# Factorization-machine kernel: squares and their weighing one quad later, and a ring of 6 quads instead of 8

## The reference

```python
gathered = jax.vmap(lambda table, idx: table[idx], in_axes=(0, 1), out_axes=1)(emb, xi)
e = gathered * xv[:, :, None]
s = jnp.sum(e, axis=1)
qi = 0.5 * (s * s - jnp.sum(e * e, axis=1))
h = jax.nn.relu(xv @ W1 + b1)
x = jnp.concatenate([qi, h], axis=1)
return x @ W2 + b2
```

## Time and profile before

| | |
|---|---|
| median of 3 runs | 752.67 us (750.71 to 755.29) |
| the profiled execution, its own time | 753.14 us |
| its span, first to last instruction | 751.3 us |
| gathers on GpSimd | 512, 508.3 us busy |
| scales on ScalarE | 512, 323.1 us busy |
| squares on ScalarE (L194) | 66, 224.7 us busy |
| weighings on VectorE (L327) | 128, 276.8 us busy |
| HBM read | 131.72 MB, 175 GB/s over the span |

### The profile page before, as it was taken

How to read it: one execution, slowest core, us unless ns; L and a number is a source line. 1 busy time by engine, 2 the same in 40 slices (tenths; PEclk the granted TensorE clock), 3 DMA queues, 4 the chain that set the end, 5 groups by cost and what they waited for, 6 DMA issues and landing times.

```text
span 751.3 us, 2355 instructions
## 1 busy us (share of the span) xinstructions
PE 98.3 (13%) x222; PEld 24.7 (3%) x222; DVE 550.3 (73%) x458; ACT 547.9 (73%) x595; POOL 509.8 (68%) x524
## 2 busy tenths in 40 slices
PE   1002020200200200202020200201102020200205
PEld 0000000000000000000000000000000000000001
DVE  3487877667567667897977577667886679767798
ACT  3687887757585676999867576676977589757693
POOL 6777777777765656677777775657777667776620
PEclk9999999999999999999999999999999999999997
DMA  7676767777765556576767765556676566766620
GB/s 226 181 203 186 202 190 202 202 193 202 198 176 139 154 147 180 153 204 181 203 194 203 202 187 152 157 146 188 167 203 185 164 176 183 202 185 171 170 64 2
DMA packets 33684, 131.92 MB, mean 176 GB/s; under 512 B 8642, under 2 KB 8770, under 8 KB 33635
## 3 DMA queue, kind: packets, MB, share of 16 engines
q0 software_dynamic: 32768, 130.06, 62.7%
q1 hardware_dynamic: 800, 1.31, 0.6%
q10 hardware_dynamic: 98, 0.40, 0.2%
HBM read 131.72 MB, written 0.01 MB: 175 GB/s over the span
## 4 chain that ended last, share of the span: by engine, by line
POOL 33%; ACT 29%; issue 26%; another core or an unknown queue 5%; DVE 5%; DMA 1%; PE 1%; POOLq 0%; ACTq 0%; DVEq 0%
POOL gathered L172 33%; ACT gathered L188 19%; ACT squares L194 9%; DVE running_ps L336 3%; DVE squares L327 2%; PE sum_ps L235 1%; ACT sum_squared L201 1%; DMA gathered<-emb,index_rows 0%; DVE added_up L336 0%; DMA index_raw<-index 0%; DVE weighted L313 0%; POOLq L168 0%; PE hidden_ps L277 0%; DVE y L437 0%
## 5 line engine op out<-in xcount | busy, mean ns | idle before, releaser
L172 POOL DMA_INDIRECT gathered<-emb,index_rows x512 | 508.3, 993 | 208.4 <-issue 155.1
L188 ACT ACTIVATE gathered<-gathered,values 128x496 f32<-128x496 f32 x512 | 323.1, 695 | 72.6 <-issue 44.7
L327 DVE SCALAR_TENSOR_TENSOR squares<-squares,w_ps 128x1984 f32<-128x1984 f32 (+1 forms) x128 | 276.8, 2165 | 42.0 <-remote 27.3
L194 ACT ACTIVATE squares<-gathered 128x3968 f32<-128x3968 f32 (+1 forms) x66 | 224.7, 3405 | 107.4 <-remote 65.1
L336 DVE SCALAR_TENSOR_TENSOR running_ps<-gathered,running_ps 128x1984 f32<-128x1984 f32 x80 | 178.2, 2227 | 88.2 <-ACT gathered L188 50.0
L235 PE MATMUL sum_ps<-added_up,own_sample 128*32 128x496 f32 x128 | 32.9, 1031 | 613.7 <-issue 494.3
L254 PE MATMUL hidden_ps<-w_b,value_rows 33*128 33x512 f32 x64 | 60.4, 1097 | 11.2 <-DVE value_rows L370 11.2
L336 DVE SCALAR_TENSOR_TENSOR added_up<-gathered,running_ps 128x1984 f32<-128x1984 f32 (+1 forms) x19 | 35.8, 1892 | 26.6 <-remote 17.7
L391 DVE SCALAR_TENSOR_TENSOR weighted_hidden<-hidden_ps,w_all 128x1024 f32<-128x1024 f32 x16 | 19.6, 1223 | 28.6 <-remote 20.6
L336 DVE SCALAR_TENSOR_TENSOR running_ps<-gathered 128x1984 f32<-128x1984 f32 x16 | 35.7, 2231 | 5.7 <-issue 3.4
L235 PEld LDWEIGHTS sum_ps<-added_up,own_sample 128*32 128x32 f32 x128 | 4.1, 139 | 640.7 <-issue 597.2
(11 more groups left out here) (27 smaller groups left out, 9.1 us busy)
## 6 DMA issues: line engine op xcount, KB each, us to landing
gathered<-emb,index_rows POOLq DMA_INDIRECT x512
w_all<-w SPq DMA_DIRECT2D x1, 760.0 KB
values<-value SPq DMA_DIRECT2D x1, 256.0 KB, 2.9
value_rows<-value_t ACTq DMA_DIRECT2D x1, 256.0 KB
index_raw<-index SPq DMA_DIRECT2D x1, 240.0 KB, 4.9
w_b<-w ACTq DMA_DIRECT2D x1, 128.0 KB
index_raw<-index SPq DMA_DIRECT2D x1, 16.0 KB, 2.7
w_b<-b ACTq DMA_DIRECT2D x1, 4.0 KB
```

The lines of the kernel that those rows point to most:

```text
L172: nc.gpsimd.indirect_dma_start(out=gathered[:, n % slots, j, :], out_offset=None, in_=emb, in_offset=bass.IndirectOffsetOnAxis(ap=index_ro ...
L188: return nc.scalar.mul(rows_of_one, rows_of_one, values[:, g:g + 1])
L194: return nc.scalar.activation(squares[:, s // deep, kept, groups], gathered[:, held, groups], ACT.Square)
L327: return nc.vector.scalar_tensor_tensor(of, of, -0.5, w2_ps[:, 0:dim].unsqueeze(1).to_broadcast([P, quads_of.stop - quads_of.start, dim]), ...
```

## The change

The ring holds 6 quads instead of 8. ScalarE squares a pair of quads after the odd quad that follows it instead of the even one: quads `n - 3` and `n - 2` after the scale of quad `n`. VectorE begins to weigh a half's squares after the second quad of the next half instead of the first, so the fourth weighing of a half falls behind the first quad of the half after next. The square of a block's field sum moves from behind quad s = 3 to behind s = 4.

```diff
--- before.py
+++ after.py
@@ -28,7 +28,7 @@
     in_block = quads * GROUPS
     halves = hidden // 512
     pairs = 2
-    slots = 8
+    slots = 6
 
     deep = quads // 2
     all_quads = blocks * quads
@@ -202,21 +202,25 @@
                                      ACT.Square).then_inc(sum_squared_ready, 1)
 
             act.wait_ge(values_loaded, 16)
+            def square_pair(n):
+                if n % deep == 0 and n >= quads:
+
+                    act.wait_ge(normed, n // deep - 1)
+                act.wait_ge(scaled, n + 2)
+                square(n, 2, slice(0, GROUPS)).then_inc(squared, 1)
+
             for n in range(all_quads - 1):
                 i, s = n // quads, n % quads
                 act.wait_ge(fetched[n % slots], (n // slots + 1) * 16 * GROUPS)
                 for j in range(GROUPS):
                     last = scale(n, j)
                 last.then_inc(scaled, 1)
-                if n % 2 == 0 and n > 0:
-
-                    if (n - 2) % deep == 0 and n - 2 >= quads:
-
-                        act.wait_ge(normed, (n - 2) // deep - 1)
-                    act.wait_ge(scaled, n)
-                    square(n - 2, 2, slice(0, GROUPS)).then_inc(squared, 1)
-                if s == 3 and i > 0:
+                if n % 2 == 1 and n > 2:
+
+                    square_pair(n - 3)
+                if s == 4 and i > 0:
                     square_sums(i - 1)
+            square_pair(all_quads - 4)
             act.wait_ge(scaled, all_quads - 1)
             square(all_quads - 2, 1, slice(0, GROUPS)).then_inc(squared, 1)
             for half in range(pairs):
@@ -372,31 +376,40 @@
             step(nc.vector.tensor_copy(w2_ps[:, 0:dim], w2_all[:, 0:dim]))
             dve.wait_ge(values_loaded, 16)
 
-            for i in range(blocks):
-                for half in range(2):
-                    first = i * quads + half * deep
-
-                    i_of, half_of = (i, 0) if half else (i - 1, 1)
-                    for t in range(deep if i + 1 < blocks or half == 0 else deep - 1):
-                        add_quad(first + t)
-                        if first > 0:
-                            if t == 0:
-                                dve.wait_ge(squared, first // 2)
-                            last = weigh_squares(i_of, half_of, t, slice(0, deep),
-                                                 norms[:, i_of, half_of, t:t + 1])
-                            if t == deep - 1:
-                                last.then_inc(normed, 1)
-                        if half == 0 and t == 0:
-                            dve.wait_ge(hidden_ready, i + 1)
-                            nc.vector.scalar_tensor_tensor(
-                                weighted_hidden[:], hidden_ps[:], 0.0,
-                                w2_all[:, dim:].rearrange("p (h c) -> p h c", h=halves),
-                                ALU.max, ALU.mult, accum_out=hidden_part[:, i:i + 1]
-                                ).then_inc(hidden_used, 1)
-                        if half == 1 and t == 0 and i > 0:
-                            weigh_sums(i - 1)
-            weigh_squares(blocks - 1, 0, deep - 1, slice(0, deep), norms[:, blocks - 1, 0, deep - 1:deep]
-                          ).then_inc(normed, 1)
+            def weigh_half(h, j):
+                i, half = divmod(h, 2)
+                last = weigh_squares(i, half, j, slice(0, deep), norms[:, i, half, j:j + 1])
+                if j == GROUPS - 1:
+                    last.then_inc(normed, 1)
+
+            for h in range(2 * blocks):
+
+
+                i, half = divmod(h, 2)
+                first = h * deep
+                add_quad(first)
+                if h > 1:
+                    weigh_half(h - 2, 3)
+                if half == 0:
+                    dve.wait_ge(hidden_ready, i + 1)
+                    nc.vector.scalar_tensor_tensor(
+                        weighted_hidden[:], hidden_ps[:], 0.0,
+                        w2_all[:, dim:].rearrange("p (h c) -> p h c", h=halves),
+                        ALU.max, ALU.mult, accum_out=hidden_part[:, i:i + 1]).then_inc(hidden_used, 1)
+                add_quad(first + 1)
+                if h > 0:
+                    dve.wait_ge(squared, first // 2)
+                    weigh_half(h - 1, 0)
+                if half == 1 and i > 0:
+                    weigh_sums(i - 1)
+                add_quad(first + 2)
+                if h > 0:
+                    weigh_half(h - 1, 1)
+                if h < 2 * blocks - 1:
+                    add_quad(first + 3)
+                if h > 0:
+                    weigh_half(h - 1, 2)
+            weigh_half(2 * blocks - 2, 3)
 
 
             end = blocks - 1
```

## The result

The changed kernel took 743.24 us (median of 4 runs, 742.78 to 743.66) against 752.83 (4 runs) of the kernel before: a ratio of 0.987, 95% interval 0.984 to 0.990. That is 1.3% less. It holds for the chip of these runs; on another chip, further down, the sign is the opposite.

What follows compares the result with a forecast made beforehand. No engine was full; a hidden queue serving one quad per about 5.6 us was taken to set the pace. Last issue 712.8, tail 31 and 1.8 around the span gave 745.6, forecast as 745 us; range 728 to 780.

Steps and rivals of the forecast that it cites:

- Issue of quad 127 as before, 712.8: GpSimd's first gather of the last quad was to start at 712.8 us, unchanged by the edit.
- The fixed mean of 5.6: Over undisturbed and disturbed stretches together, a quad takes about 5.6 us on average, whatever the lengths of the stretches.
- Squares a quad later, gain nothing: ScalarE's double squares, moved behind a later scale, save nothing, though the trace charges 65.1 us to their waits.
- The ring, cost nothing, 1.5 us to spare: With 6 slots, three quads of lead (15.0 us) cover the 13.5 us from gather to squares' end; GpSimd loses nothing.
- The chain of 13.5 us: From a quad's issue through its scale and squares to GpSimd's reaction: 13.25 plus 0.24 us.
- Tail 31: From the last quad's issue to the span's end: 31 us instead of 38.5, between 28 and 35.
- Scales 1.40 us apart remain: In disturbed stretches ScalarE's scales would still start 1.40 us apart instead of 0.60.
- the queue: Hidden queue, unidentified: fills while gathers run at 5.15 us per quad, drains at 6.47, with a service of about 5.6.
- The late announcements: ScalarE's finished work becomes known late: scales recorded done by 451.1, VectorE's add of that quad starting only at 459.19.
- rival A: The moved waits before ScalarE's squares cause the late announcements; without them GpSimd runs undisturbed: 689 us, chance 0.12.
- Rival B: The shorter ring becomes the bound, with 5.8 us per quad or more: 776 us, slower, chance 0.23.
- the trace contradicts: Against the skill's rule that semaphores update at an instruction's recorded end: scales end by 451.1, the add starts at 459.19.

Runs made afterwards that it cites:

- the kernels meant to tell: Three differences to the changed kernel, on chip 5: 16 useless matmuls per block, one scale per quad, gathers of half rows; 689.59, 690.86 and 692.63 us.
- the one with the old end: Changed kernel with the old order of squares and weighings in its last half alone, on chip 13: 689.34 us, ratio 1.0078 to the kernel before.

## Why the prediction was right, and what it did not know

The time (745, measured 743.2) and the sign came out as forecast. By its own steps, for the chip of its profile:

- **Issue of quad 127 as before, 712.8**: measured 714.0. The fixed mean of 5.6 held in the new trace (5.62) and, by the last issue, for rings of 6 and 8 in either order and of 10 in the new one. This was the step that the forecast hung on, and it held. In the new trace the mean stays within 5.61 and 5.62 for every 8 quads from 204 to 699 us.
- **Squares a quad later, gain nothing**: right. The new order alone gives 0.9996, although 68 of the 107 us of idle before the squares are gone in its trace. What is left there are 38 gaps of at most 1.4 us.
- **The ring, cost nothing, 1.5 us to spare**: right in both conditions. On chip 7, with the new order, a release falls into GpSimd's gap four times, and it loses nothing, for the gap is 0.3 us there as anywhere. The chain of 13.5 us behind it is well sized: with the ring of 4 two quads take 13.9.
- **Tail 31**: 27.9, so this term was 3.1 us too long. The scale of 127 stands 10.85 us behind the issue; I had taken the middle of 9.1 to 16.2, and the run ended near the lower end. From that scale to the end are 17.1 us, where the term had 16.75 and 2.14 for a third weighing, 18.9. It's partly luck that the sum is within 2 us: the issue came 1.2 us later than taken, the tail was 3.1 us shorter, and the two errors offset each other in part.
- **Scales 1.40 us apart remain**: wrong. There is none left in the new trace, where the one before has 38 scales that start 1.3 to 1.5 us behind the scale ahead of them. The announcements are late all the same (83 of 91 adds). It takes both parts: 25 such scales are left with the old order and the ring of 6, and 69 with the new order and the ring of 8. My reading is that GpSimd, held back sooner, lets ScalarE wait for data instead; no run tests it. The spacing of scales is one face of the queue, not the queue.
- **The late announcements as a property of the kernel**: this premise was never said, and it is what failed, though the forecast came true where it was made. All rows were of one profile. On chips 5, 7 and 13 the same kernel takes 683 to 685 us, and the change is 1.1% slower on the one where both were timed. The text even had the number, as rival A: 689 against a measured 690.3. A's pace was right for an undisturbed GpSimd (issue 659, measured 661.9), its tail was too long (28, measured 24.3), so the near hit is partly luck, and its cause was wrong. The new order does not remove the late announcements (0.9996 on chip 6); on the other chips they were never there.
- **Rival B** fails with 6 slots: 5.62 us per quad, not 5.8. With 4 it is what happens. More slots were no help either: 10 give 760.1.
- The sentence that **the trace contradicts** the Trainium skill (Perfetto Trace Analysis, DVE / Act Engine Instruction) holds only where announcements are late. On chip 7, and with the ring of 4 on chip 6, an add starts 0.03 us after the recorded end, as the rule says.

**Where the cost on the other chips comes from.** Last issue +1.1 and tail +2.7 are the 3.9 us between the two spans on chip 7 (the profiled execution of the changed kernel is the fastest of its four; the medians are 5.65 us apart). The tail holds the third weighing behind the add of 126, which the prediction had as 2.14; the add itself starts 0.65 us later behind the last issue. The add of 126 and the last weighing behind it, in the kernel before:

```profile
666.04 2.22 DVE L336 SCALAR_TENSOR_TENSOR running_ps<-gathered,running_ps 128x1984 f32<-128x1984 f32 x1
...
670.32 2.22 DVE L327 SCALAR_TENSOR_TENSOR squares<-squares,w_ps 128x1984 f32<-128x1984 f32 x1
```

In the changed kernel:

```profile
667.78 2.22 DVE L340 SCALAR_TENSOR_TENSOR running_ps<-gathered,running_ps 128x1984 f32<-128x1984 f32 x1
...
674.19 2.22 DVE L331 SCALAR_TENSOR_TENSOR squares<-squares,w_ps 128x1984 f32<-128x1984 f32 x1
```

The +1.1 comes from the long gathers.

**Which version to take.** The ring of 6 with the old order: 0.990 where announcements are late, 1.0004 where they are not. The change as made: 0.987 and 1.011. In the first case the reordering may bring some 2 us more (743.2 against 745.5), which isn't shown: the two were timed in different groups, and the intervals of their ratios overlap (0.984 to 0.990 and 0.987 to 0.9925). In the second it costs some 5 us by the medians (ratios of 1.0112 and 1.0004, whose intervals lie apart).

**Still open.** What the queue is (recording or something else), whether the chip or the hour decides it (each named chip was used in one group only), and what feeds it: the kernels meant to tell ran where it doesn't occur, and the question wasn't tried again.

## What to carry to other kernels

A wait whose releaser the profile can't name, with the other engine's recorded end several microseconds earlier, is a reason to take the same profile on another chip before tuning around it. Where the middle keeps a fixed mean whatever the ring, as here with 6, 8 and 10 slots, a deeper ring only lets the queue in front of the tail grow. So look at the time from the last issue to the end. Split a change with several parts: here one part made the gain and was free elsewhere, the other cost.

## What the runs showed of the hardware

**The long gather has a cause.** The prediction took one gather in 32 to be longer by itself. In the fourteen traces, long gathers are the ones that begin while one particular pass of VectorE runs: the first add of a block, which reads **two** operands from SBUF (`running_ps<-gathered`, without `running_ps` as an input). There are 217 of them for 224 such passes (four traces have one more, of 1.3 to 1.4 us, in GpSimd's first microseconds of gathering). Each ends 0.81 or 0.82 us after the pass. Beside the other seven passes, with rings of 8 and 10 slots and the new order, GpSimd happened to be waiting, and its next gather, 0.1 us behind the pass, takes 0.95 us. In the changed kernel on chip 7, at two places:

```profile
185.41 2.23 DVE L340 SCALAR_TENSOR_TENSOR running_ps<-gathered 128x1984 f32<-128x1984 f32 x1 [0.31 <-ACT gathered L188]
185.45 3.00 POOL L172 DMA_INDIRECT gathered<-emb,index_rows  x1 [0.30 <-issue]
...
227.54 2.24 DVE L340 SCALAR_TENSOR_TENSOR running_ps<-gathered 128x1984 f32<-128x1984 f32 x1 [0.49 <-ACT gathered L188]
228.77 1.82 POOL L172 DMA_INDIRECT gathered<-emb,index_rows  x1 [0.30 <-issue]
```

The pass ends at 187.64 and the gather at 188.45; then 229.78 and 230.59, 0.81 us both times. A gather that starts right behind the pass's start takes 3.0 us, one that starts late in it 1.8. Weighings and the other adds, with their second operand in PSUM, run beside gathers of 0.95 us. The Trainium skill (SBUF — State Buffer, SBUF: two separate sides) says that a VectorE instruction with two SBUF inputs and a GpSimd one that reads SBUF exclude each other for the whole instruction, the later one waiting. For the pass the traces agree: gathers that begin 0.05 us or more after the pass has begun are held until it ends. For the gather they show less: 17 that begin at most 0.02 us before or 0.04 us after the pass's start take 0.95 us, and the pass becomes only 0.01 to 0.07 us longer than its 2.23, not by the length of the gather.

This sets where the last issue stands without late announcements. The 16 block gathers are 2.24 us on average in the old order on chip 7, 2.34 in the changed kernel and 2.47 in the one with the old end. The last pair is 2 us for 16, most of the 2.7 us between these two last issues; as such a gather can take anything from 1.4 to 3.0, it may also be why the changed kernel's runs scatter over 8 us there. Even at 2.24 the collisions cost GpSimd 16 x (2.24 − 0.95) = 21 us of the 661 in which it is the bound. In the first two profiles they average 2.39 and 1.62 us, which is 12 of the 13 us by which the changed kernel's gathers are shorter there; it gained nothing by that, since its mean per quad was set elsewhere. A first add that reads one operand from PSUM might avoid them; it wasn't tried.
